# A recurrent layer on one core: gate biases spread by TensorE, the second pair's first input products placed between the gates, and each weight matrix loaded in two halves by two issuers

## The reference, cut to what matters

```python
x = x + _L0_cond_ref(x, cond_1024, ...)          # x: (16, 512, 512) fp32; batch 16, 512 steps, 512 channels

Xz = jnp.einsum('btc,hc->tbh', X, Wxz) + bxz     # the same for Xr, Xh
def step(H, xs):
    xz, xr, xh = xs
    Z = jax.nn.sigmoid(xz + H @ Whz.T + bhz)
    R = jax.nn.sigmoid(xr + H @ Whr.T + bhr)
    H_tilda = jnp.tanh(xh + R * H @ Whh.T + bhh)
    H_new = Z * H + (1.0 - Z) * H_tilda
    Y = H_new @ Whq.T + bhq
    return (H_new, Y)
_, Ys = jax.lax.scan(step, h0, (Xz, Xr, Xh))     # 512 steps one after the other
```

## Time and profile before

| | |
|---|---|
| three timed runs | 2160.05, 2160.69, 2160.74 us; median 2160.69 |
| the profiled execution, its own time | 2159.91 us |
| its span | 2158.1 us, granted TensorE clock 0.999 |
| TensorE (PE) busy | 2142.6 us, 99% of the span |
| VectorE (DVE), ScalarE (ACT), GpSimd (POOL) busy | 1621.6, 844.8, 167.3 us |
| loads and stores | 62.68 MB, mean 29 GB/s |

### The profile page before, as it was taken

The page is one execution under the profiler, slowest core; times in us unless marked ns, Lnnn a source line. Parts: engine busy times, 40 slices in busy tenths (PEclk is TensorE's granted clock), DMA queues, the critical chain, the costliest instruction groups (busy, mean ns, idle before and its releaser), DMA issues.

```text
span 2158.1 us, 193479 instructions
## 1 busy us (share of the span) xinstructions
PE 2142.6 (99%) x85184; PEld 2131.3 (99%) x85184; DVE 1621.6 (75%) x9469; ACT 844.8 (39%) x4864; POOL 167.3 (8%) x520
## 2 busy tenths in 40 slices
PE   7999999999999999999999999999999999999999
PEld 7999999999999999999999999999999999999998
DVE  5777777777777777777777777777777777777777
ACT  2333433343334333433343334333343334333333
POOL 1000000000000000000000000000000000000000
PEclk9999999999999999999999999999999999999999
DMA  4010001000000000000000010001000000010000
GB/s 160 26 29 24 24 26 28 24 24 26 27 26 24 25 27 26 24 24 27 28 24 24 26 29 24 24 26 29 24 24 26 29 24 24 26 29 24 24 26 27
DMA packets 111764, 62.68 MB, mean 29 GB/s; under 512 B 28800, under 2 KB 110848, under 8 KB 110976
## 3 DMA queue, kind: packets, MB, share of 16 engines
q1 hardware_dynamic: 111744, 62.37, 9.9%
HBM read 45.55 MB, written 16.78 MB: 29 GB/s over the span
## 4 chain that ended last, share of the span: by engine, by line
PE 99%; DVE 1%; DMA 0%; issue 0%; ACT 0%; SPq 0%
PE gates L396 61%; PE p_bank L321 16%; PE gates L321 12%; PE y_bank L329 10%; DMA bias_in<-in_b_gate 0%; DVE pre_t L628 0%; DVE scanned L692 0%; DVE t L735 0%; DVE t L749 0%; DVE reset_state L731 0%; PE p_bank L428 0%; DVE yt L683 0%; ACT scan_on L614 0%; PE y_bank L371 0%; ACT gates L620 0%
## 5 line engine op out<-in xcount | busy, mean ns | idle before, releaser
L396 PE MATMUL gates<-wh,scanned 128*16 128x128 f32 x32768 | 1047.4, 273 | 3.9 <-DVE scanned L692 2.3
L396 PEld LDWEIGHTS gates<-wh,scanned 128*16 128x16 f32 x32768 | 935.7, 104 | 5.8 <-DVE scanned L692 3.1
L628 DVE STREAM_TRANSPOSE pre_t<-gates 128x32 f32<-128x32 f32 (+2 forms) x3584 | 618.1, 216 | 209.5 <-PE gates L396 157.3
L396 PE MATMUL gates<-wh,reset_state 128*16 128x128 f32 (+1 forms) x16384 | 600.4, 273 | 1.9 <-issue 1.6
L396 PEld LDWEIGHTS gates<-wh,reset_state 128*16 128x16 f32 (+1 forms) x16384 | 471.6, 103 | 5.2 <-issue 2.6
L599 ACT ACTIVATE r_gate<-pre_t 128x16 f32<-128x16 f32 (+1 forms) x1536 | 234.6, 215 | 511.6 <-DVE pre_t L628 511.6
L321 PE MATMUL p_bank<-t,s 128*32 128x192 f32 x7112 | 361.7, 303 | 0.0
L614 ACT ACTIVATE scan_on<-pre_t 128x16 f32<-128x16 f32 (+1 forms) x1536 | 238.1, 218 | 267.0 <-DVE pre_t L628 267.0
L692 DVE TENSOR_TENSOR_SCAN scanned<-scan_by,scan_on 128x32 f32<-128x32 f32 x2048 | 300.9, 210 | 28.6
L321 PEld LDWEIGHTS p_bank<-t,s 128*32 128x32 f32 x7112 | 284.9, 110 | 2.8
L746 DVE TENSOR_TENSOR scan_on<-z_gate,scanned 128x64 f32<-128x64 f32 x512 | 116.4, 227 | 174.1 <-ACT z_gate L603 174.1
(11 more groups left out here) (76 smaller groups left out, 1571.7 us busy)
## 6 DMA issues: line engine op xcount, KB each, us to landing
xr<-in_x_t SPq DMA_DIRECT2D x128, 128.0 KB, 2.1
y_io<-in_x_res SPq DMA_DIRECT2D x256, 64.0 KB, 2.0
out<-y_io SPq DMA_DIRECT2D x256, 64.0 KB, 1.6
x_b<-in_x_t SPq DMA_DIRECT2D x127, 32.0 KB, 1.7
wx_v<-in_w_xv SPq DMA_DIRECT2D x1, 1536.0 KB, 6.6
wx_u<-in_w_xu SPq DMA_DIRECT2D x1, 1536.0 KB, 11.7
wh<-in_w_hr SPq DMA_DIRECT2D x1, 1024.0 KB, 13.0
wh<-in_w_hz SPq DMA_DIRECT2D x1, 1024.0 KB, 14.9
```

The source lines that it names most:

```text
L396: mm = nc.tensor.matmul(gate_rows(g, par, slice(Q * j, Q * j + rows)), of, w, start=False, stop=(m == G - 1), skip_group_check=True)
L628: nc.vector.transpose(flat(pre_t[g][:, a:b]), gate_part(g, par, a, b)).then_inc(done, 1)
```

## The change

Four things change. First, the biases are loaded as 2 partitions by ScalarE, and TensorE multiplies them with a tensor of ones, which spreads them over the rows of the gate banks and adds the two vectors; ScalarE then copies one bank back to `bias_rows`. Second, x of turn 0 has its own buffer `x_first`; the products of pair 0 stay ahead of turn 0, those of pair 1 stand between the gates of step 0 in the place of `keep_busy`. Third, each of wx_v, wx_u, wh0, wh1 and wh2 is loaded in two halves, the lower (`0:half`) issued by SyncE, the upper (`half:G`) by ScalarE. Fourth, t4 is made in two halves, in steps 0 and 1, and `project_y` waits for the parts of the state one by one.

```diff
-            load_xr(0)
-            sp.dma_start(wx[0][:], w_x[0]).then_inc(wx_loaded[0], 16)
-            sp.dma_start(bias_in[:], b_gate).then_inc(bias_loaded, 16)
-            sp.dma_start(wx[1][:], w_x[1]).then_inc(wx_loaded[1], 16)
-            sp.dma_start(h0_in[:], h0).then_inc(h0_loaded, 16)
-            for g in range(3):
-                sp.dma_start(wh[g][:], w_h[g]).then_inc(wh_loaded[g], 16)
-            sp.wait_ge(xr_used, 1)
+            for n in range(2):
+                sp.dma_start(wx[n][:, 0:half], w_x[n][:, 0:half]).then_inc(wx_loaded[n], 16)
+            for g in (R, Z):
+                sp.dma_start(wh[g][:, 0:half], w_h[g][:, 0:half]).then_inc(wh_loaded[g], 16)
+            sp.dma_start(wh[H][:, 0:half], w_h[H][:, 0:half]).then_inc(wh_loaded[H], 16)
             load_xr(1)
             load_xb(1)
-            sp.wait_ge(wh_loaded[H], 16)
+            sp.wait_ge(wh_upper_loaded, 16)
...
@@ tensor @@
+            def first_products(par, n):
+                pe.wait_ge(wx_loaded[n], 32)
+                for m in range(G):
+                    if n == 1:
+                        products(gates[par], H_AT, x_first[:, par], wx[1], m, ALL)
+                    else:
+                        for cols in (WIDE, NARROW):
+                            products(gates[par], Z_AT, x_first[:, par], wx[0], m, cols)
...
                 recur(R, i, 0, first)
                 if first:
-                    keep_busy(4)
+                    pe.wait_ge(bias_ready, 1)
+                    first_products(1, 0)
                 recur(Z, i, 0, first)
                 if first:
-                    keep_busy(5)
+                    first_products(1, 1)
...
-            pe.wait_ge(x_filled, 2)
-            pe.wait_ge(xr_loaded, 16)
-            pe.wait_ge(wx_loaded[0], 16)
+            pe.wait_ge(ones_ready, 1)
+            pe.wait_ge(bias_loaded, 16)
             for par in range(2):
-                for m in range(G):
-                    for cols in (WIDE, NARROW):
-                        products(gates[par], Z_AT, xr[:, par], wx[0], m, cols)
+                for at, cols in ((Z_AT, P), (512, 2 * P)):
+                    for j in range(G):
+                        mm = nc.tensor.matmul(gates[par][Q * j:Q * (j + 1), at:at + cols], ones[:],
+                                              bias_in[:, j, at - Z_AT:at - Z_AT + cols], start=True, stop=True)
+            mm.then_inc(biases_in, 1)
+            pe.wait_ge(x_first_loaded, 16)
+            first_products(0, 0)
             keep_busy(6)
-            pe.wait_ge(wx_loaded[1], 16)
-            for par in range(2):
-                for m in range(G):
-                    mm = products(gates[par], H_AT, xr[:, par], wx[1], m, ALL)
-            mm.then_inc(xr_used, 1)
+            first_products(0, 1)
...
@@ scalar @@
-            for par in range(2):
-                nc.scalar.copy(gates[par][:, Z_AT:Z_AT + 2 * W], bias_rows[:].rearrange("p a c -> p (a c)")
-                               ).then_inc(x_filled, 1)
+            act.dma_start(bias_in[:], b_gate).then_inc(bias_loaded, 16)
+            act.dma_start(x_first[:], x_t[0]).then_inc(x_first_loaded, 16)
+            act.dma_start(h0_in[:], h0).then_inc(h0_loaded, 16)
+            for n in range(2):
+                act.dma_start(wx[n][:, half:G], w_x[n][:, half:G]).then_inc(wx_loaded[n], 16)
+            for g in (R, Z):
+                act.dma_start(wh[g][:, half:G], w_h[g][:, half:G]).then_inc(wh_loaded[g], 16)
+            act.dma_start(wh[H][:, half:G], w_h[H][:, half:G]).then_inc(wh_upper_loaded, 16)
+            act.wait_ge(biases_in, 1)
+            nc.scalar.copy(bias_rows[:].rearrange("p a c -> p (a c)"), gates[1][:, Z_AT:Z_AT + 2 * W]
+                           ).then_inc(bias_ready, 1)
...
@@ vector, step c of turn 0 @@
-                        nc.vector.tensor_tensor(w_sum[3][:], wx[0][:, half:G], w_sum[1][:], ALU.subtract
+                    if first and c < half:
+                        nc.vector.tensor_tensor(w_sum[3][:, c], wx[0][:, half + c], w_sum[1][:, c], ALU.subtract
                                                 ).then_inc(t_ready[3], 1)
...
@@ tensor, project_y and its last call @@
                 for m in range(G):
+                    for h, (a, _) in enumerate(PARTS):
+                        if m == a:
+                            pe.wait_ge(state_ready[h], 2 * pairs - 1 + 2 * par)
...
-            for h in range(N):
-                pe.wait_ge(state_ready[h], 2 * pairs + 1)
             project_y(1).then_inc(y_projected, 1)
```

More of the change, by code:

```diff
@@ L60, in gru @@
         w_sum = [sb(f"t{n}", [P, half, CW]) for n in range(1, 5)]
-        bias_in = sb("bias_in", [P, 2, 2, W])
+        bias_in = sb("bias_in", [2, G, 2 * W])
+        ones = sb("ones", [2, Q])
         bias_rows = sb("bias_rows", [P, 2, W])
@@ L66, in gru @@
         xr = sb("xr", [P, 2, G, Q])
+        x_first = sb("x_first", [P, 2, G, Q])
         x_b1 = sb("x_b1", [P, half, Q])
@@ L113, in gru @@
         bias_loaded = sem("bias_loaded")
+        biases_in = sem("biases_in")
         bias_ready = sem("bias_ready")
@@ L116, in gru @@
         h0_ready = sem("h0_ready")
-        banks_primed = sem("banks_primed")
-        x_filled = sem("x_filled")
+        ones_ready = sem("ones_ready")
+        x_first_loaded = sem("x_first_loaded")
         p5_filled = sem("p5_filled")
@@ L222, in turn @@
                 if not last:
[L224 removed]
+                    sp.wait_ge(xr_used, i)
                     sp.wait_ge(s3_ready, i)
@@ L379, in recur @@
                 if first and c == 0:
-                    pe.wait_ge(wh_loaded[g], 16)
+                    pe.wait_ge(wh_loaded[g], 16 if g == H else 32)
                 for m in range(G):
+                    if first and c == 0 and g == H and m == half:
+                        pe.wait_ge(wh_upper_loaded, 16)
                     for h, (a, _) in enumerate(PARTS):
@@ L529, in _ @@
             pe.wait_ge(zeros_ready, 1)
-            for to, at in ((gates[0], Z_AT), (gates[0], 512), (gates[1], Z_AT), (gates[1], 512), (y_bank, 0), (p5_bank, 0)):
+            for to, at in ((y_bank, 0), (p5_bank, 0)):
                 for j in range(G):
                     nc.tensor.matmul(to[Q * j:Q * (j + 1), at:at + P], zeros[:, 0:Q], zeros[:], start=True, stop=True)
-            for to, at in ((gates[0], 512), (gates[1], 512), (p5_bank, 0), (y_bank, 0), (y_bank, P), (y_bank, 2 * P)):
+            for to, at in ((p5_bank, 0), (y_bank, 0), (y_bank, P), (y_bank, 2 * P)):
@@ L534, in _ @@
                 for j in range(G):
-                    mm = nc.tensor.matmul(to[Q * j:Q * (j + 1), at + P:at + 2 * P], zeros[:, 0:Q], zeros[:], start=False,
-                                          stop=True, skip_group_check=True)
-            mm.then_inc(banks_primed, 1)
-            pe.wait_ge(x_filled, 2)
-            pe.wait_ge(xr_loaded, 16)
-            pe.wait_ge(wx_loaded[0], 16)
-            for par in range(2):
-                for m in range(G):
-                    for cols in (WIDE, NARROW):
-                        products(gates[par], Z_AT, xr[:, par], wx[0], m, cols)
@@ L546, in _ @@
-            keep_busy(6)
-            pe.wait_ge(wx_loaded[1], 16)
-            for par in range(2):
-                for m in range(G):
-                    mm = products(gates[par], H_AT, xr[:, par], wx[1], m, ALL)
-            mm.then_inc(xr_used, 1)
+                    nc.tensor.matmul(to[Q * j:Q * (j + 1), at + P:at + 2 * P], zeros[:, 0:Q], zeros[:], start=False,
+                                     stop=True, skip_group_check=True)
+            pe.wait_ge(ones_ready, 1)
+            pe.wait_ge(bias_loaded, 16)
@@ L755, in turn @@
                         renew(t, h, par, s)
-            dve.wait_ge(bias_loaded, 16)
-            nc.vector.tensor_tensor(bias_rows[:], bias_in[:, 0], bias_in[:, 1], ALU.add).then_inc(bias_ready, 1)
-            dve.wait_ge(wx_loaded[0], 16)
-            dve.wait_ge(wx_loaded[1], 16)
+            dve.wait_ge(bias_ready, 1)
+            dve.wait_ge(wx_loaded[0], 32)
+            dve.wait_ge(wx_loaded[1], 32)
             nc.vector.tensor_tensor(w_sum[0][:], wx[1][:, 0:half], wx[0][:, 0:half], ALU.subtract
@@ L813 @@
         "h0": _np.asarray(inputs["cond_1024"]).T.reshape(P, G, batch),
-        "b_gate": _np.stack([in_rows(in_vu(*(by_block(bias(a + g)) for g in "rzh"))).reshape(P, 2, -1)
-                             for a in ("bx", "bh")], axis=1),
+        "b_gate": _np.stack([in_vu(*(by_block(bias(a + g)) for g in "rzh")) for a in ("bx", "bh")]),
         "b_out": in_rows(bias("bhq")),
```

10 lines of the change are left out of this document (5 added, 5 removed).

## The result

Six runs of the changed kernel took 2172.89 to 2174.53 us, median 2173.82, against 2160.55 before (six runs): ratio 1.0061, 95% interval 1.0051 to 1.0072. The prediction said 2158.0 with a range of 2155.5 to 2160.7: wrong, and on the side to which it gave 0.04. The profiled execution took 2172.89 us, 12.98 more than the one of before; its span is 2171.1.

The account below looks back on a forecast made before the run. TensorE was taken to bound the turns, so only start and end could shorten: -3.2 (H turned earlier) + 0.4 (step 1) + 0.5 (turn 1) - 0.4 (tail) = -2.7 us, giving 2158.0 on the median, range 2155.5 to 2160.7.

Parts of the forecast that it names:

- Rival E: Loop's code: body touches one block more; if not all stay, 2.25 us each pass, 284 us, 2444 in all; chance 0.04.
- (a): Start, weight loads: wx_u complete at 14.1 us, between bounds of 13.0 and 16.7.
- rival C: Start: upper halves come last, wx_u at 16.7, R at 18.8, H ends at 24.7; 2159.6 us; chance 0.13.
- (b): Step 0, R's start: after t1, at 16.2 us and not 18.70, so 2.5 earlier.
- rival D: Clock: after idling TensorE may run at the lower level from R to H, +1.9 us: 2159.9; chance 0.06.
- (c): Step 0, R to the end of H: a block's edge stalls TensorE 1.65 us near Z's end; H ends at 23.0.
- (d): VectorE in step 0: with only half of t4 there, H is turned at 23.1 and not 26.28, -3.2 us.
- (e): Step 1: half of t4 costs +0.1 us, a block's edge in Z +0.3.
- (f): Turn 1, first pass through the loop: six block edges fall into the way, not five, +0.5 us (0 to 0.8).
- (g): Tail: the last project_y starts once the first of four scans is done, -0.4 us (0 to 0.5).

Follow-up runs that it names:

- e3: The kernel before with 21 zero products more, so that its loop's head stands 4 instructions ahead of a block edge: 2174.69 us.
- e2: The changed kernel with 2 groups of zero products fewer, its loop's head 37 instructions ahead of the edge, still touching seven blocks: 2160.0 us.
- e5: e1 with x and h0 issued by SyncE ahead of the weight halves, which keep their two issuers: 2159.22 us.
- e10: e9 with the last two residual blocks loaded into a buffer of their own before the last turn: 2155.75 us.
- e11: e10 with 8 zero products more early in the wait for the loads: 2156.71 us.
- e1: The changed kernel with 4 zero products more ahead of the biases, moving the loop's head past the block edge: 2161.23 us.
- e12: The changed kernel with two zero products more, so that the block edge stands 3 instructions ahead of the loop's head: 2161.07 us.
- e4: e1 with each weight matrix whole again, issued by SyncE with x and h0 in the old order, ScalarE issuing only the biases: 2157.61 us.
- e9: e4 with 16 zero products more early in the wait for the loads, every block edge 32 records earlier: 2157.20 us.
- e8: e4 with pair 1's products ahead of turn 0 again and zero products between the gates: 2160.19 us.

## Why the prediction was wrong

- **The loop.** This is the step that failed: "a gain can only be a shorter start or end", with no term for the later passes in the sum. (Nor does the change leave the loop quite as it was: TensorE's body has 1343 instructions and not 1344, a register operation fewer; e3 shows that this is not the cause.) Rival E, "if these did not all stay, each pass would pay as the first did, 2.25 us", names the loop but not the mechanism: the prediction priced the loop's code at a refetch or at nothing, and saw only how many blocks the body touches. The blocks did stay, and e2 shows that their number costs nothing. What costs is where the head stands in its block: 0.097 us a pass, 12.0 in all, three times the 0.034 at which the prediction itself said that this side decides. Its last sentence, "wrong if the turns get another pace than 16.63", is what happened. The Trainium skill, "Runtime: NRT & Kernel Launch", Instruction fetch mechanics, says that a taken branch whose target is not in the current two pages forces a fetch, though it also gives TensorE room for 2048 instructions, more than the loop has; here the loop jumps back over five blocks, and 16 packets in the whole execution show no fetch, only the 0.1 us.
- **(a)** wx_u was complete at 16.1, not 14.1: near rival C's 16.7, though for another reason (e5: small pieces ahead in the queue). That wx_v, too, waits for its upper half, 13.17 where the whole tensor was there at 7.8 before (6.6 us after its issue at 1.2), has no term in the sum, and it is what R's start hung on.
- **(b)** R started at 20.28, not 16.2, and t1 did not bind: TensorE's 144 records from 13.30 on took 7.0 us. wx_v's 64 took 44 ns each (e10: 1.53/64 = 24), the 48 zeros 53 ns (27 before). In e11, where TensorE had not idled, R started 4.0 us after wx_v's first product (12.71 and 16.67), here 6.7 (13.30 and 20.01). It looks like rival D in a place where the prediction did not look, for TensorE idled 6.8 us ahead of 13.30; but the granted clock in this trace reads 1.00 there, so that it was the clock is not shown.
- **(c)** The stall in Z was 0.37, not 1.65, because R came late and the block did not: it was usable at 23.63, 3.4 us after R's start, where the sum allowed 3.6 to 5.5. That makes 5.8 us from R's start to H's end against 6.8 in the prediction. Place right, size not.
- **(d)** H was turned at 26.24, not 23.1 (26.28 before): VectorE's lateness is gone as predicted, and the start ate it.
- **(e), (f)** Turn 1's sum came 0.8 later than before with H turned at the same time, and the first pass another 1.2: +0.4 and +0.5 were forecast. The passes of turns 0 and 1 ran from 16.42 to 18.29 and from 18.88 to 21.05 us over these kernels, which the count of edges alone does not explain.
- **(g)** The tail gave 1.0, not 0.4. The last products start 0.28 after the first of the four last scans (2166.87 and 2167.15); the waits are right. Behind them the reload became the bound, which the prediction did not see.

Without the loop's 12.0 the sum would have been off as well: e1, e2 and e12, the changed kernel off the edge, took 2160.0 to 2161.2 us, the same as before within their intervals, where 2158.0 was forecast.

## What to carry to other kernels

A loop that runs often can be sensitive to where its head lies in the instruction stream, here by 0.1 us of a pass of 16.6: before a change ahead of a loop is judged, compare the pace of the passes, and if it moved with no instruction in the body changed, shift the head by a few harmless instructions and time again. Splitting each load over two issuers delayed here what was needed first, most of all where small pieces stood ahead of a half; judge such a split by when the whole tensor is there. When a tail gets shorter, read what its chain hangs on next: here a store and a reload of one buffer.

## What the runs showed of the hardware

- A block edge 4, 5 and 13 instructions behind a loop's head costs 0.110, 0.097 and 0.030 us a pass; 37 or more behind, or 3 or 11 ahead, nothing. Why the cost falls off within these distances (a block made ready again after the jump) is argued, not shown.
- With two data queues, 128 KB of x landed 6.5 us after its issue behind nothing but 12 KB in its own queue, and 32 KB of h0 7.7; alone ahead on SyncE (e4) x took 2.1.
- wx_v's 64 records took 2.79 us in the changed kernel, e4 and e5, and 1.53 in e9 and e10, where TensorE had been at zeros right before. The windows over them (busy of each engine, granted clock, DMA share, GB/s), changed kernel and then e4:

```profile
13.30:16.09 2.79, 2.79 (x70) 2.79 (x74) 0.00 (x0) 0.00 (x0) 0.00 (x0) 1.00 1.00 408
```

```profile
7.80:10.50 2.70, 2.70 (x68) 2.70 (x72) 0.00 (x0) 0.47 (x1) 0.00 (x0) 0.50 1.00 423
```

In e4 the granted clock is 0.50, 1.2 GHz, after idling. In the changed kernel the pace is the same and the record reads 1.00; that its clock was low too is likely, and its trace does not show it.
- A block's edge in step 0 cost 0.20 us of weight loads and no idle time of the products (e1, in Z), 0.37 us (changed kernel) or 3.03 (e8), and 0.57 or 2.16 in two kernels that are the same up to the last turn. What decides within that stays open.
